# A drain on GpSimd behind every second row gather of a three-layer graph network

## The chip, the core and the metric

The kernel runs on one core of a Trainium2 chip. The metric is the device time of one execution in microseconds (us); lower is better. Engines in the profile: PE is TensorE (PEld its weight loads), DVE is VectorE, ACT is ScalarE, POOL is GpSimd, SP is SyncE. A q behind an engine's name means its sequencer alone.

## The reference

6250 nodes with 256 features each, 100,000 edges sorted by target node, an edge type from 0 to 2, and 32 attributes per edge. Cut to what matters:

```python
ew = edge_attr @ edge_w + edge_b                      # (E, 256)
inv_cnt[i] = 1 / max(segment_sum(edge_type == i, dst), 1)
for l in range(3):
    residual = x
    msg = relu(x[src] * ew)                           # gather one row of x per edge
    out = 0
    for i in range(3):                                # edge types
        h = segment_sum(msg * (edge_type == i), dst) * inv_cnt[i]
        out += h @ weights[l, i]
    x = residual + relu(out + x @ roots[l] + biases[l])
return layernorm(x_input + x)
```

Every layer gathers 100,000 rows of 1 KB from the x that the layer before has written. No layer can start its gathers before the last rows of x are stored.

## The kernel before, in words

The edges are cut into 782 tiles of 128 edges. One tile is one gather: a single indirect DMA, issued by GpSimd, that takes 128 row numbers from `idx` and brings 128 rows of 256 float32 from HBM into one of 12 slots of the tile `xg` in SBUF. Two tiles make a pair, and the pair is the step of the loop: 391 pairs per layer, 1173 in all, 2346 gathers.

For each pair q the engines do this, in this order:

- PE computes the edge factors of both tiles into PSUM (line 781, four matmuls with 128x256 outputs).
- DVE multiplies the gathered rows by them in place (line 1088). It waits first for the two gathers of the pair (one semaphore per slot, `s_g`) and for PE (`s_e`).
- ACT applies relu in place (line 685).
- PE sums the messages per node and type with one-hot selectors `S` (line 800, eight records per pair), and counts the tile as used on the semaphore `s_sc`.
- DVE adds the two results to the running sums `acc` (line 971).

When the sums of a block of 128 nodes are complete (49 blocks per layer), PE multiplies them with the layer's weights (line 849), DVE adds bias, means and residual (lines 988, 995, 1013), and SP stores the new rows (line 541). Layer 0 also transposes the edge attributes and counts edges; layer 2 also does the layernorm.

No scheduler is at work: each engine runs its own hand-written program, and semaphores join them. GpSimd's program is nearly nothing but gathers. The gather n waits until the tile n-12, which had its slot, has been used by line 800; that wait has the same value for both gathers of a pair, so only the first of them can be held by it. Twelve gathers are issued ahead of the branch into the main loop, then come a few memsets (lines 615 to 622), then the others. At the start of layers 1 and 2 GpSimd waits for the stores of x (`s_xo`, line 628).

In the same queue as the gathers there is nothing else. The other transfers (edge attributes, node blocks, weights, stores) are issued by SP.

Of the kernel before, what the change touches and what calls it, by code (L numbers as in the profile page):

```python
# [59 lines left out]
def gnn_program(nc, x_in, src, dst, edge_attr, edge_type, weights, roots, biases, edge_w, edge_b, due, out):  # L60
# [30 lines left out]
    xs = [x_in, x1, x2, out]  # L91

    order, _, _, blocks, starts, first = plan()

    def rows(k):
# [12 lines left out]
    with ctx:  # L108
# [60 lines left out]
        def c3(p):  # L169
            return p.rearrange("q (c p) -> q c p", p=128)  # L170
# [42 lines left out]
        def uses(l, i, depth, per):  # L213

            return len(range(i, l * per, depth))

        def tile(n):

            return 4 * order[n // 4] + n % 4
# [246 lines left out]
        def both(eng, name, fast):  # L466

            eng.wait_ge(s_flag, 4)
            late = eng.value_load(flag[0:1, 0:1], min_val=0, max_val=128 * 128 * CH + 128 * CH)
            with eng.If(late == 0):  # L470
                fast()
            with eng.Else():
                general(eng, name)
# [112 lines left out]
        @block.gpsimd  # L586
        def _(eng):
            eng.memset(c3(p_src)[:, CH - 1, :], 0).then_inc(s_pad, 1)
            eng.memset(c3(p_dst)[:, CH - 1, :], PAD).then_inc(s_pad, 1)
            eng.memset(c3(p_typ)[:, CH - 1, :], 0).then_inc(s_pad, 1)  # L590
            eng.memset(zcol[:, :], 0.0).then_inc(s_zc, 1)
            eng.memset(p_ew, 0.0).then_inc(s_ez, 1)
            eng.memset(ident[:, :], 0.0).then_inc(s_id, 1)
            eng.wait_ge(s_id, 1)
            eng.affine_select(out=ident[:, :], in_=ident[:, :], compare_op=ALU.not_equal, fill=1.0,
                              base=0, pattern=[[-1, 128]], channel_multiplier=1).then_inc(s_id, 1)
            eng.iota(iota[:, :], [[1, 148]], base=-1, channel_multiplier=0,
                     allow_small_or_imprecise_dtypes=True).then_inc(s_cst, 1)
            eng.memset(ones[:, :], 1.0).then_inc(s_cst, 1)
            eng.memset(mask[:, :], HIGH).then_inc(s_cst, 1)  # L600
            eng.memset(eps[:, :], 1e-5).then_inc(s_cst, 1)
            eng.memset(accf[:, Z[0]:Z[1]], 0.0).then_inc(s_z0, 1)

            def gather(l, j):
                n = l * NT + j
                if n >= XR:
                    eng.wait_ge(s_sc, 2 * ((n - XR) // 2 + 1))
                eng.indirect_dma_start(  # L608
                    out=xg[:, n % XR, :], out_offset=None, in_=xs[l],
                    in_offset=bass.IndirectOffsetOnAxis(ap=idx[:, tile(j):tile(j) + 1], axis=0)).then_inc(s_g[n % XR], 16)  # L610

            eng.wait_ge(s_idx, 2)
            for j in range(XR):
                gather(0, j)
            eng.memset(diff[:, :], 0.0).then_inc(s_df, 1)
            for i, (fill, b) in enumerate(((0.5, 0), (-0.5, 1), (0.5, -127))):
                eng.wait_ge(s_df, i + 1)
                eng.affine_select(out=diff[:, :], in_=diff[:, :], compare_op=ALU.not_equal, fill=fill,
                                  base=b, pattern=[[-1, 128]], channel_multiplier=1).then_inc(s_df, 1)
            eng.memset(accf[:, Z[4]:Z[5]], 0.0).then_inc(s_z0, 1)  # L620
            eng.wait_ge(s_pc, 3)
            eng.memset(accf[:, Z[5]:Z[6]], 0.0).then_inc(s_z0, 1)

            def fast():
                for l in range(L):
                    if l:
                        for i in range(TB):
                            eng.wait_ge(s_xo[i], 16 * uses(l, i, TB, NB))
                    for j in range(0 if l else XR, NT):
                        gather(l, j)  # L630

            both(eng, "gpsimd", fast)
# [245 lines left out]
        def _(eng):  # L878
# [191 lines left out]
            def fast():  # L1070
                for l in range(L):
                    todo = {}
                    for q in range(-6, end):
                        Q = l * NP + q
                        if 0 <= q < NP and q % 2 == 0:
                            w, c = min(4, NT - 2 * q), tile(2 * q)
                            row, c = 32 * (c // BR), c % BR
                            _, vals = nc.values_load_multi_w_load_instructions(  # L1078
                                brow[row:row + 1, c:c + w], engines=[DVE], min_val=0, max_val=R * (N - 1),
                                skip_runtime_bounds_check_because="three times a node's number")  # L1080
                            bases.update({2 * q + i: v for i, v in enumerate(vals)})
# [59 lines left out]
```

## Time and profile before

| what | us |
|---|---|
| median of 3 timed runs | 3098.7 |
| lowest and highest of them | 3095.48, 3101.99 |
| profiled execution, first to last instruction (span) | 3632.0 |
| PE busy in the span | 2818.6 |
| POOL busy in the span | 2256.5 |
| DVE busy in the span | 2148.2 |
| ACT busy in the span | 1285.0 |

The span is all that is recorded of the profiled execution's own time; what lies around it isn't given. It is 533 us longer than the median of the timed runs. Every duration of a single instruction comes from that slower execution. Busy time is the sum of an engine's instruction spans; for a gather, POOL's span is the writing of the transfer's descriptors, not the transfer. Waits are listed as idle time before an instruction, with what ended it; "issue" means that nothing which the profile shows was waited for.

### The profile page before, as it was taken

The numbers are of one execution on the slowest core, as the hardware profiler recorded it, in microseconds if no ns is written. First come the engines' busy times: TensorE is split into PE (matmuls) and PEld (weight loads), VectorE is DVE, ScalarE is ACT, GpSimd is POOL, SyncE is SP. The second block draws the span as 40 slices with busy tenths as digits, with TensorE's granted clock in tenths as the row PEclk, the third lists the DMA queues.
The fourth block names the chain that finished last, engine by engine and source line by source line (L and its number), as shares of the span: only waits on it lengthen the run. The fifth ranks groups of instructions, "written<-read, shape, count | busy, mean of one in ns | idle before, by whom it ended". The sixth has DMA issues, their size and how long they took to land.

```text
span 3632.0 us, 59677 instructions
## 1 busy us (share of the span) xinstructions
PE 2818.6 (78%) x18430; PEld 2609.9 (72%) x18430; DVE 2148.2 (59%) x5997; ACT 1285.0 (35%) x2700; POOL 2256.5 (62%) x2368
## 2 busy tenths in 40 slices
PE   6777778888888777778777877777777777787777
PEld 5777777777777677777777777767666777777776
DVE  6666666666666555555555555545555665556566
ACT  6555555555555322222222222222222222222222
POOL 6666666666666466666666666646666666666664
PEclk9999999999999878888898888887888888888888
DMA  4444444444444344444444444434444444444443
GB/s 126 128 129 128 127 132 127 131 127 131 130 128 130 114 125 118 122 119 121 122 124 118 124 122 119 122 106 127 125 126 121 130 123 127 129 124 130 125 128 100
DMA packets 318631, 450.88 MB, mean 124 GB/s; under 512 B 155996, under 2 KB 205802, under 8 KB 318314
## 3 DMA queue, kind: packets, MB, share of 16 engines
q0 software_dynamic: 112608, 307.65, 29.8%
q1 hardware_dynamic: 205706, 139.36, 13.7%
q8 instruction: 156, 2.56, 0.3%
q14 instruction: 161, 1.32, 0.1%
HBM read 401.96 MB, written 44.82 MB: 123 GB/s over the span
## 4 chain that ended last, share of the span: by engine, by line
PE 61%; issue 16%; another core or an unknown queue 9%; DVE 8%; ACT 3%; DVEq 2%; POOL 1%; DMA 0%; POOLq 0%; SPq 0%
PE bank L800 31%; PE bank L781 14%; PE bank L849 13%; DVE acc L971 4%; PE bank L754 2%; DVE t L988 1%; DVE xg L1088 1%; ACT at L656 1%; PE bank L824 1%; ACT oh_a L702 1%; PE bank L795 1%; DVEq L1078 1%; DVEq L971 1%; DVE S L952 0%
## 5 line engine op out<-in xcount | busy, mean ns | idle before, releaser
L608 POOL DMA_INDIRECT xg<-x,idx x1564 | 1490.9, 953 | 897.3 <-issue 361.5
L800 PE MATMUL bank<-S,xg 128*128 128x96 f32 x9384 | 1459.0, 305 | 400.7 <-issue 197.4
L800 PEld LDWEIGHTS bank<-S,xg 128*128 128x128 f32 x9384 | 1324.2, 217 | 461.2 <-issue 441.2
L685 ACT ACTIVATE xg<-xg 128x512 f32<-128x512 f32 x1173 | 739.1, 630 | 2064.0 <-DVE xg L1088 1270.0
L971 DVE TENSOR_TENSOR acc<-acc,bank 128x192 f32 x2346 | 817.1, 348 | 767.0 <-PE bank L800 490.6
L1088 DVE TENSOR_TENSOR xg<-xg,bank 128x512 f32<-128x512 f32 x1173 | 802.0, 684 | 600.2 <-remote 273.5
L781 PE MATMUL bank<-wsb,at 128*128 128x256 f32 x4692 | 990.4, 338 | 213.8 <-issue 128.8
L608 POOL DMA_INDIRECT xg<-in_x_dram,idx x782 | 750.5, 960 | 451.0 <-PE bank L800 212.2
L781 PEld LDWEIGHTS bank<-wsb,at 128*128 128x128 f32 x4692 | 753.8, 214 | 286.7 <-issue 183.5
L849 PE MATMUL bank<-W,acc 128*128 128x256 f32 x1764 | 506.5, 411 | 2.2 <-issue 2.0
L849 PEld LDWEIGHTS bank<-W,acc 128*128 128x128 f32 x1764 | 385.5, 257 | 5.6 <-issue 2.0
L952 DVE TENSOR_TENSOR S<-iota,kr 128x384 f32<-128x384 bf16 x588 | 324.4, 552 | 0.2
L702 ACT ACTIVATE oh_a<-iota,lo 128x128 bf16<-128x128 bf16 x782 | 267.6, 389 | 69.3 <-PE bank L800 62.8
L988 DVE SCALAR_TENSOR_TENSOR t<-bank,inv,t 128x256 f32<-128x256 f32 x441 | 209.8, 476 | 19.2 <-remote 14.7
L849 PE MATMUL bank<-W,xT 128*128 128x256 f32 (+1 forms) x588 | 195.0, 464 | 0.0
L754 PE MATMUL bank<-ident,hs 128*64 128x128 f32 x782 | 126.1, 284 | 45.8 <-issue 40.4
L795 PE MATMUL bank<-oh_b,oh_a 128*128 128x12 bf16 x782 | 80.0, 174 | 101.1 <-issue 98.2
L795 PEld LDWEIGHTS bank<-oh_b,oh_a 128*128 128x128 bf16 x782 | 52.0, 105 | 132.3 <-issue 113.8
L849 PEld LDWEIGHTS bank<-W,xT 128*128 128x128 f32 (+1 forms) x588 | 125.7, 234 | 14.2 <-issue 0.3
L754 PEld LDWEIGHTS bank<-ident,hs 128*64 128x64 f32 x782 | 86.7, 122 | 58.0 <-issue 56.1
L656 ACT ACTIVATE at<-bank 64x512 fp32r<-64x512 f32 x196 | 113.1, 577 | 42.3 <-remote 32.7
L709 ACT ACTIVATE acc<-zcol 128x768 f32<-128x768 f32 (+1 forms) x98 | 81.7, 834 | 37.3 <-remote 21.7
(87 smaller groups left out, 728.2 us busy)
## 6 DMA issues: line engine op xcount, KB each, us to landing
at<-attr_t SPq DMA_DIRECT2D x390, 128.0 KB
xg<-x,idx POOLq DMA_INDIRECT x1564
attr_t<-at SPq DMA_DIRECT2D x195, 128.0 KB
xg<-in_x_dram,idx POOLq DMA_INDIRECT x782
hs<-in_edge_attr_dram SPq DMA_DIRECT2D x195, 64.0 KB
x<-t SPq DMA_DIRECT2D x96, 128.0 KB
xblk<-x SPq DMA_DIRECT2D x96, 128.0 KB
xblk<-in_x_dram SPq DMA_DIRECT2D x48, 128.0 KB
```

The source lines that it names most:

```text
L608: eng.indirect_dma_start(out=xg[:, n % XR, :], out_offset=None, in_=xs[l], in_offset=bass.IndirectOffsetOnAxis(ap=idx[:, tile(j):tile(j) + ...
L685: eng.activation(v, v, ACT.Relu).then_inc(s_r, 1)
L702: eng.activation(oh_a[:, j % AR, :], iota[:, 1:129], ACT.Sign, bias=lo[:, tile(j):tile(j) + 1]).then_inc(s_oh, 1)
L754: last = eng.transpose(pT[0:64, 128 * i:128 * i + 128], hs[:, g % 3, i, :], ident[:, :])
L781: last = eng.matmul(pE[Q % 2][:, 256 * i:256 * i + 256], at[:, sl, c:c + 128], wsb[:, p, :], start=(p == 0), stop=(p == 1))
L795: eng.matmul(pA[V % 2][:, 384:384 + HW], oh_a[:, (2 * V + i) % AR, :], oh_b[:, slot(l, 2 * q + i), :], start=(i == 0), stop=(i == 1))
L800: last = eng.matmul(pA[V % 2][:, 192 * i + 96 * h:192 * i + 96 * h + 96], xg[:, n % XR, 128 * h:128 * h + 128], S[:, slot(l, 2 * q + i), : ...
L849: last = eng.matmul(o, a, W[:, 2 * (r % 4) + h, :], start=(h == 0), stop=(h == 1))
L952: eng.tensor_tensor(S[:, at4:at4 + w, :], iota[:, 1:WK + 1].unsqueeze(1).to_broadcast([128, w, WK]), kr[:, c:c + w].unsqueeze(2).to_broadc ...
L971: eng.tensor_tensor(a, a, pA[V % 2][:, 192 * i:192 * i + 192] .rearrange("p (h w) -> p h w", h=2), ALU.add).then_inc(s_acc, 1)
L988: return eng.scalar_tensor_tensor(tt, products(k, m), inv[0:n, 3 * blocks[k] + r:3 * blocks[k] + r + 1], tt, ALU.mult, ALU.add)
L1088: eng.tensor_tensor(v, v, pE[Q % 2][:, :].rearrange("p (i d) -> p i d", i=2), ALU.mult).then_inc(s_m, 1)
```

## The change

GpSimd's `gather` gets two lines. Behind every gather with an odd running number, thus once per pair, GpSimd executes a drain instruction. It is not tied to any semaphore. Nothing else is altered; no instruction moves on any engine, and the other engines' programs are the same.

```diff
                 eng.indirect_dma_start(
                     out=xg[:, n % XR, :], out_offset=None, in_=xs[l],
                     in_offset=bass.IndirectOffsetOnAxis(ap=idx[:, tile(j):tile(j) + 1], axis=0)).then_inc(s_g[n % XR], 16)
+                if n % 2:
+                    eng.drain()
 
             eng.wait_ge(s_idx, 2)
             for j in range(XR):
```

The line numbers of the profile are those of the kernel before; the added lines stand behind line 610. `gather` is called for the twelve gathers ahead of the main loop too, so there are 1173 drains: six ahead of the memsets of lines 615 to 622, and 1167 behind them.

## Rows read from the trace of the kernel before

**Rows 1.** The page, busy time of each engine in the whole span.
```profile
PE 2818.6 (78%) x18430; PEld 2609.9 (72%) x18430; DVE 2148.2 (59%) x5997; ACT 1285.0 (35%) x2700; POOL 2256.5 (62%) x2368
```

**Rows 2.** POOL's waits: who waited for whom, us in total, times, longest.
```profile
POOL xg L608 <- issue: 537.8, 1749, 0.7
POOL xg L608 <- PE bank L800: 466.7, 409, 2.3
POOL xg L608 <- remote: 295.2, 185, 2.9
POOL xg L608 <- DMA x<-t: 45.0, 2, 23.1
```

**Rows 3.** Timeline of POOL in layer 1: start, duration, instruction, idle before.
```profile
2004.20 0.95 POOL L608 DMA_INDIRECT xg<-x,idx  x1 [0.30 <-issue]
2005.45 0.95 POOL L608 DMA_INDIRECT xg<-x,idx  x1 [0.30 <-issue]
2006.70 0.95 POOL L608 DMA_INDIRECT xg<-x,idx  x1 [0.30 <-issue]
2008.98 0.94 POOL L608 DMA_INDIRECT xg<-x,idx  x1 [1.33 <-PE bank L800]
2010.23 0.95 POOL L608 DMA_INDIRECT xg<-x,idx  x1 [0.30 <-issue]
```

**Rows 4.** Timeline of DVE at the end of layer 2.
```profile
3605.29 0.68 DVE L1088 TENSOR_TENSOR xg<-xg,bank 128x512 f32<-128x512 f32 x1
3607.15 0.69 DVE L1088 TENSOR_TENSOR xg<-xg,bank 128x512 f32<-128x512 f32 x1
3609.20 0.68 DVE L1088 TENSOR_TENSOR xg<-xg,bank 128x512 f32<-128x512 f32 x1
3611.05 0.69 DVE L1088 TENSOR_TENSOR xg<-xg,bank 128x512 f32<-128x512 f32 x1 [0.25 <-issue]
```

**Rows 5.** Timeline of POOL around the first turn of a layer.
```profile
1217.01 0.94 POOL L608 DMA_INDIRECT xg<-in_x_dram,idx  x1 [0.30 <-issue]
1239.81 0.94 POOL L608 DMA_INDIRECT xg<-x,idx  x1 [21.86 <-DMA x<-t]
1241.06 0.95 POOL L608 DMA_INDIRECT xg<-x,idx  x1 [0.30 <-issue]
1242.31 0.95 POOL L608 DMA_INDIRECT xg<-x,idx  x1 [0.30 <-issue]
1243.56 0.95 POOL L608 DMA_INDIRECT xg<-x,idx  x1 [0.30 <-issue]
1244.82 0.95 POOL L608 DMA_INDIRECT xg<-x,idx  x1 [0.30 <-issue]
1246.07 1.04 POOL L608 DMA_INDIRECT xg<-x,idx  x1 [0.30 <-issue]
```

**Rows 6.** Timeline of DVE behind it: the layer's first three multiplies.
```profile
1245.13 0.69 DVE L1088 TENSOR_TENSOR xg<-xg,bank 128x512 f32<-128x512 f32 x1 [10.34 <-DMA xg<-x,idx]
...
1246.40 0.69 DVE L1088 TENSOR_TENSOR xg<-xg,bank 128x512 f32<-128x512 f32 x1
1248.94 0.69 DVE L1088 TENSOR_TENSOR xg<-xg,bank 128x512 f32<-128x512 f32 x1 [1.85 <-DMA xg<-x,idx]
```

**Rows 7.** Instructions of the program's end: count, duration in ns, start.
```profile
L108 POOLq DRAIN  x1: 10670/10670/10670, 3603.9 to 3603.9; - x1
L108 PEldq DRAIN  x1: 68/68/68, 3620.4 to 3620.4; - x1
L108 ACTq DRAIN  x1: 164/164/164, 3624.2 to 3624.2; - x1
```

**Rows 8.** Timeline of POOL at the program's end.
```profile
3605.18 0.94 POOL L608 DMA_INDIRECT xg<-x,idx  x1 [0.30 <-issue]
```

**Rows 9.** Instructions of the program's first line: count, duration in ns, start.
```profile
L1128 POOLq DRAIN  x1: 187/187/187, 0.4 to 0.4; - x1
```

**Rows 10.** Timeline of POOL before and behind the memsets.
```profile
12.32 1.22 POOL L608 DMA_INDIRECT xg<-in_x_dram,idx  x1 [3.72 <-DVE idx L903]
...
28.95 0.22 POOL L615 MEMSET diff<- 128x128 f32 x1
...
36.94 0.96 POOL L608 DMA_INDIRECT xg<-in_x_dram,idx  x1 [0.15 <-issue]
```

**Rows 11.** Timeline of PE at the start of layer 1.
```profile
1245.96 1.20 PE L781 MATMUL bank<-wsb,at 128*128 128x256 f32 x4 [3.58 <-DVE xg L1088]
1246.96 1.85 PE L800 MATMUL bank<-S,xg 128*128 128x96 f32 x8
```

**Rows 12.** The page, costliest groups: count, busy us, mean ns, idle before.
```profile
L849 PE MATMUL bank<-W,acc 128*128 128x256 f32 x1764 | 506.5, 411 | 2.2 <-issue 2.0
...
L849 PE MATMUL bank<-W,xT 128*128 128x256 f32 (+1 forms) x588 | 195.0, 464 | 0.0
L754 PE MATMUL bank<-ident,hs 128*64 128x128 f32 x782 | 126.1, 284 | 45.8 <-issue 40.4
L795 PE MATMUL bank<-oh_b,oh_a 128*128 128x12 bf16 x782 | 80.0, 174 | 101.1 <-issue 98.2
```

## The prediction, made before the changed kernel had run

> **What bounds the kernel now.** I read the page's busy times first [rows 1]. There PE looks like the bound with 78%, and POOL with 62% seems to have room. That view misleads here, because a gather's 0.95 us is not all that it costs POOL. The timeline of POOL shows it [rows 3]: gathers that wait for nothing start 1.25 us apart, 0.95 us of writing descriptors and 0.30 us of idle time called "issue", so the shortest period of a pair is 2.50 us. The profiled execution takes some 3.0 us per pair, and the waits tell where the rest goes [rows 2]: in 409 + 185 cases POOL waited for PE or for an unnamed releaser, 762 us in all, and 45 us for stores at the two turns of a layer. So in the profile POOL is held by the 12 slots, and the consumers set the pace.
>
> The timed runs are 533 us shorter than the span. I take away what isn't pairs: 12.3 us until the first gather, 8.0 us of memsets (28.95 to 36.94) [rows 10], two turns of 21.9 us [rows 5] and 25.9 us behind the last gather (3632.0 - 3606.1) [rows 8]. That leaves 3098.7 - 90 = 3009 us for 1173 pairs, 2.56 us each. This is 0.06 us over POOL's own 2.50 us. The consumers can be faster than that: at the end of layer 2, where all rows are there, multiplies follow each other in 1.86, 2.05 and 1.85 us [rows 4]. So in the timed runs POOL's queue is nearly saturated, and whatever is put into it counts in full past 0.06 us per pair; in the profiled execution past some 0.5 us.
>
> **The change, and what one drain costs.** It adds 1173 drains and moves nothing. Behind each drain in POOL's queue stands the next pair of gathers, and for them wait DVE's multiply, then ACT, PE and the sums. The question is what the drain waits for. No drain stands behind a gather in a loop in this trace, so I bound it by the three rows that are nearest.
>
> - Lower bound: the drain at the program's start [rows 9] took 187 ns, and all of POOL's work there was memsets of some 0.1 us. A drain that costs the queue only the time of an empty one: 0.05 to 0.19 us.
> - Landing: the drain waits until the rows of both gathers have arrived. How long that is can be read at the start of layer 1, where DVE waits for the rows. The second pair's gather ends at 1243.56 + 0.95 = 1244.51 and its multiply starts at 1246.40, 1.89 us later. The third pair's ends at 1247.11 and its multiply starts at 1248.94, 1.83 us later. The first pair takes 1245.13 - 1242.01 = 3.12 us, with the layer's other loads under way [rows 5, 6]. I take 1.85 us.
> - Upper bound: the closing drain of POOL ran from 3603.9 for 10.67 us, until 3614.5 [rows 7]. The last gather had finished its descriptors at 3606.1 [rows 8], and nothing but drain stood in the queue. So this drain waited 8.4 us behind the last descriptors. The drains of PE and ACT at the same place took 68 and 164 ns [rows 7], so it is not the place that makes it long.
>
> The closing drain is the only one behind gathers, and it excludes that a POOL drain ends with the descriptors: it stayed at least as long as rows need to land. It stayed 6.5 us longer still (8.4 - 1.9), and why I can't read. It came behind 2346 gathers with no drain between, the drains of the change come behind two. I read the excess as settling what had piled up, and expect next to nothing of it behind a single pair. That is the weakest choice here.
>
> The Trainium skill speaks against this. Its page Perfetto Trace Analysis, section DMA Instruction — SWDGE (GPSIMD), lets the GpSimd instruction complete when its cores have written the descriptors, before the data moves; a drain that waits for the engine's instructions alone would by that rule return at once. VectorE: DVE Perf Modes, section The DRAIN you can't avoid, calls the drains around a program boilerplate of about 12 ns on all five engines. By these two the sum would stay at 3098.7 us. The closing drain of 10.67 us does not agree with either.
>
> **The sum.** Period of a pair with a drain: 1.25 us from the first gather's start to the second's, 0.95 us for the second's descriptors, 1.85 us until landing, 0.05 us for the drain to notice, and 0.35 us until the next gather starts (the 0.30 us of issue, and 0.05 us since it can't be prepared during the wait). That is 4.45 us. The slots don't hold POOL then: 12 of them cover 6 pairs, and the consumers need 2 us for what arrives every 4.45. Nothing hides the wait, because the drain stops the very queue that sets the pace.
>
> 1173 x 4.45 = 5220 us. Around it: 12.3 us until the first gather, 8.0 us of memsets. The turns: today 21.86 us between the last descriptors of a layer and the next gather [rows 5]. At the end of layer 2 the last multiply starts 4.9 us behind the last descriptors (3611.05 - 3606.12) [rows 4, 8]; with the drain only 1.9 us, since no backlog is left, so a turn shrinks by 3.0 to 18.8 us, of which 2.25 us are in the pair's period already: 16.6 us, twice 33. The tail: 25.9 - 3.0 - 2.25 = 20.6 us. Sum: 5220 + 12 + 8 + 33 + 21 = 5294, and I say 5290 us. That is 1660 us over the profiled span and 2190 us over the median of the timed runs. I expect span and timed runs to lie close together this time, since what made the profiled execution slow sat with the consumers, and they have room now. The 0.95 and 1.25 us I carry over to the timed runs because their 2.56 us per pair leaves no place for a slower POOL. The landing time might be shorter without the profiler; 0.35 us less would give 4880 us. With 0.5 us more (the first pair's 3.12 us in one case of two) it is 5880 us. The forecast's own range is 4880 to 5880.
>
> **Rivals.**
>
> *The drain ends with the descriptors and hides.* It costs POOL at most the 0.06 us of room per pair, beside waits of 1.33 us for PE as at 2008.98 [rows 3]. Time 3099 us, not slower. The point from which it decides: a drain below 0.06 us. For it speaks the start's drain, most of whose 187 ns lay over the memsets; against it the closing drain. 5%, and 1% for a kernel that even gains since descriptors come in pairs with a rest.
>
> *The drain ends with the descriptors, but breaks the queue.* It costs 0.19 us [rows 9] per pair, 0.13 us past the room: 3098.7 + 1173 x 0.13 = 3250 us. 6%.
>
> *PE falls to its lower clock and becomes the bound.* PE would be busy 2 of 4.45 us and might be granted 1.2 instead of 2.4 GHz. At the start of layer 1, after its 3.58 us of idle time, four matmuls of line 781 took 1.20 us and eight of line 800 took 1.85 us [rows 11]. The blocks' matmuls are (506.5 + 195.0) / 1173 = 0.60 us per pair at the mixed clock [rows 12], up to 1.2 us at the lower: 4.25 us in layers 1 and 2, which just fits. Layer 0 adds (126.1 + 80.0) / 391 = 0.53 us, up to 1.05 us: 5.3 us, 0.85 over POOL's period, times 391 = 332 us. Total 5620 us. [...] 6%.
>
> *Every drain costs what the closing one did.* Period 1.25 + 0.95 + 8.41 + 0.35 = 10.96 us, total 12,930 us. For it speaks the only row of its kind. 4%.
>
> **Chances.** Waiting for the landing 78%, with the low clock on top 6%, 8.4 us each 4%, cheap but visible 6%, hidden 5%, gain 1%. A measurement of this kernel can tell 0.2% (6 us) from no change. So slower 94%, same 5%, faster 1%. The range 4850 to 5950 us holds the first two; I leave out the others.
>
> **What would show it.** In the profile after: 1175 POOL drains (1173 and the program's own two) with a median near 4.2 us, as the sequencer is at the drain before the gathers ahead of it have run (the closing one began at 3603.9, ahead of the gather of 3605.18 [rows 7, 8]); gathers in twos, 1.25 us apart, then 3.2 us to the next start; POOL's waits for PE gone; DVE's multiply waiting for the gather's DMA in nearly every pair, where it now does so at the layers' starts; a pair's period of 4.45 us in all three layers alike; a closing drain that has shrunk from 10.67 to about 3 us. A period that differs between layer 0 and the others would speak for PE's clock. The prediction is wrong if drains end within 0.2 us of the second gather's descriptors, or if they outlast the landing by far more than 0.1 us.

## The result, and the profile after

The changed kernel takes 6049.4 us (median of 4 runs, 6046.9 to 6051.3), the kernel before 3100.3 us in the same runs. The ratio is 1.954, 95% interval 1.951 to 1.957. Forecast were 5290 us with a range of 4850 to 5950 us: the direction and the mechanism held, the size did not.

The one profiled execution of the kernel before was itself slower than its timed runs (3632 against 3100 us), while every other kernel's profile here, of the changed one too (6049.1 us), agrees with its timed runs within 0.1%.

The page of the changed kernel: its span, the busy time of each engine and the granted clock in 40 equal slices, in tenths of full speed. They answer to [rows 1].

```profile
span 6049.1 us, 60850 instructions
PE 4052.7 (67%) x18430; PEld 3424.2 (57%) x18430; DVE 2146.5 (35%) x5997; ACT 1268.8 (21%) x2700; POOL 2234.4 (37%) x2368
...
PEclk7676766777777666666666666666566666666666
```

The clock row of the kernel before:

```profile
PEclk9999999999999878888898888887888888888888
```

POOL's, DVE's and ACT's busy times have not changed by more than 2%. POOL does the same work and stands still in between. PE's matmuls became longer, 4053 us in place of 2819 us, at a lower granted clock: 0.66 of full speed on average, where the profile of the kernel before had 0.895. Both are mixtures of the two levels, 1.2 and 2.4 GHz.

The drains of the loop: count, then shortest, median and longest duration in ns, then the first and the last start in us.

```profile
L612 POOLq DRAIN  x1173: 3421/3899/8920, 12.1 to 6023.2; - x196
```

The waits of the changed kernel: who waited for whom, us in total, times, longest. They answer to [rows 2].

```profile
ACT xg L687 <- DVE xg L1090: 4743.5, 1170, 22.6
POOL xg L608 <- issue: 3376.7, 2208, 5.5
DVE xg L1090 <- issue: 1868.3, 601, 5.4
DVE xg L1090 <- DMA xg<-x,idx: 1472.0, 409, 11.1
...
DVE xg L1090 <- DMA xg<-in_x_dram,idx: 496.6, 157, 4.1
...
POOL xg L608 <- PE bank L802: 367.3, 135, 3.6
```

DVE's multiply (now line 1090) waits 3837 us in all, in 1167 of 1173 cases, and it starts 0.08 us behind the landing of its rows in nearly all of them, also where the profile says "issue". In kernel 1 below, whose profile shows what the timed runs of the kernel before do, it waited 859 us for them, of which the largest part is this:

```profile
DVE xg L1091 <- DMA xg<-x,idx: 404.6, 370, 11.1
```

POOL's idle time ahead of gathers is put down to "issue", since a drain has no semaphore by which the profile could name it. The "PE bank L802" among POOL's waits is a trap: the sums that the gather waits for have ended at least 6.2 us before it starts (22 us in the median), and only the same semaphore happened to be updated by a later pair near the end of the drain.

One pair of the changed kernel, timeline of POOL, and of DVE behind it: start, duration, idle before. They answer to [rows 3] and [rows 6].

```profile
2810.86 0.94 POOL L608 DMA_INDIRECT xg<-x,idx  x1 [3.62 <-issue]
2812.11 0.94 POOL L608 DMA_INDIRECT xg<-x,idx  x1 [0.30 <-issue]
2815.65 0.94 POOL L608 DMA_INDIRECT xg<-x,idx  x1 [2.60 <-issue]
```

```profile
2814.89 0.69 DVE L1090 TENSOR_TENSOR xg<-xg,bank 128x512 f32<-128x512 f32 x1 [3.11 <-issue]
```

The second gather has its descriptors written at 2813.05. At 2814.89, 1.84 us later, its rows are there and DVE starts. At 2815.65, 0.76 us behind that, POOL writes again. Over all pairs the trace's records of the semaphores give the terms, as means: landing 2.05 us behind the descriptors (median 1.85, one in ten over 2.70), drain's end 0.115 us behind the landing, next gather 0.76 us behind the drain's end (median 0.73; the mean holds the two waits at the turns of a layer). The middle term is the finding: while the landing varies from 1.71 to 4.65 us, the drain's end stays 0.114 to 0.116 us behind it in nearly all pairs and 0.125 us at the most.

The program's closing drain, answering to [rows 7]:

```profile
L108 POOLq DRAIN  x1: 55/55/55, 6027.7 to 6027.7; - x1
```

It took 10.67 us before and 55 ns now, with the last pair already drained.

### The profile page after: what moved, and what is told of

Same layout as the page of the kernel before. It is cut to its first block, busy times and chain, and to the rows that moved or that the text cites. A ratio compares the mean times of both kernels' runs of the same rounds, so it can differ in the third digit from the quotient of the medians.

```text
span 6049.1 us, 60850 instructions
## 1 busy us (share of the span) xinstructions
PE 4052.7 (67%) x18430; PEld 3424.2 (57%) x18430; DVE 2146.5 (35%) x5997; ACT 1268.8 (21%) x2700; POOL 2234.4 (37%) x2368
## 3 DMA queue, kind: packets, MB, share of 16 engines
q8 instruction: 156, 2.56, 0.2%
## 4 chain that ended last, share of the span: by engine, by line
PE 29%; issue 29%; DMA 24%; POOL 7%; DVE 6%; POOLq 3%; ACT 2%; DVEq 0%
PE bank L802 17%; DMA xg<-x,idx 15%; PE bank L783 9%; DMA xg<-in_x_dram,idx 8%; POOL xg L608 7%; DVE xg L1090 5%; POOLq L612 3%; PE bank L851 2%; ACT at L658 1%; PE bank L756 1%; DVE acc L973 0%; PE bank L797 0%; PE bank L826 0%; DVEq L1088 0%; ACT xT L695 0%
## 5 line engine op out<-in xcount | busy, mean ns | idle before, releaser
L783 PE MATMUL bank<-wsb,at 128*128 128x256 f32 x4692 | 1210.3, 399 | 1562.8 <-DVE xg L1090 1338.0
L802 PE MATMUL bank<-S,xg 128*128 128x96 f32 x9384 | 1965.2, 378 | 121.8 <-DVE acc L973 75.7
L783 PEld LDWEIGHTS bank<-wsb,at 128*128 128x128 f32 x4692 | 923.2, 273 | 1936.3 <-issue 850.6
L802 PEld LDWEIGHTS bank<-S,xg 128*128 128x128 f32 x9384 | 1770.9, 282 | 216.7 <-ACT xg L687 144.6
L851 PE MATMUL bank<-W,acc 128*128 128x256 f32 x1764 | 664.8, 516 | 2.5 <-DVE t L990 2.5
L851 PEld LDWEIGHTS bank<-W,acc 128*128 128x128 f32 x1764 | 458.7, 293 | 43.7 <-DVE t L990 2.8
L851 PE MATMUL bank<-W,xT 128*128 128x256 f32 (+1 forms) x588 | 252.3, 575 | 0.0
L756 PE MATMUL bank<-ident,hs 128*64 128x128 f32 x782 | 172.6, 364 | 89.6 <-ACT xT L695 89.6
L826 PE MATMUL bank<-ident,xblk 128*128 128x128 f32 (+1 forms) x294 | 83.7, 382 | 116.7 <-ACT at L658 116.7
L826 PEld LDWEIGHTS bank<-ident,xblk 128*128 128x128 f32 (+1 forms) x294 | 53.3, 211 | 142.5 <-issue 138.5
```

The lines of the kernel that those rows point to most:

```text
L756: last = eng.transpose(pT[0:64, 128 * i:128 * i + 128], hs[:, g % 3, i, :], ident[:, :])
L783: last = eng.matmul(pE[Q % 2][:, 256 * i:256 * i + 256], at[:, sl, c:c + 128], wsb[:, p, :], start=(p == 0), stop=(p == 1))
L802: last = eng.matmul(pA[V % 2][:, 192 * i + 96 * h:192 * i + 96 * h + 96], xg[:, n % XR, 128 * h:128 * h + 128], S[:, slot(l, 2 * q + i), : ...
L851: last = eng.matmul(o, a, W[:, 2 * (r % 4) + h, :], start=(h == 0), stop=(h == 1))
```

## The experiments

Their terms are read in the same way, from the traces' semaphore records. "L" is the theory that a drain waits for the landing of the gathers ahead of it.

**Is it the landing?** First, a wait for the same landing in place of the drain.

```diff
                 if n % 2:
-                    eng.drain()
+                    eng.wait_ge(s_g[n % XR], 16 * (n // XR + 1))
```

> In place of each drain GpSimd waits on the semaphore that tells of the second gather's landing; no drain in the loop. Theory L (a drain holds the queue until the rows of the gathers before it have landed, 2.05 us behind the descriptors on average in the changed kernel, then ends 0.12 us later, and the empty queue needs 0.76 us to the next gather): the landing stays, and only the restart can be cheaper, since the next gather is prepared while it waits. Period 1.25 + 0.95 + 2.05 + 0.3 to 0.5 us = 4.55 to 4.75 us, total 5400 to 5650 us. Rival F (a drain has a fixed price of some 2.9 us of its own, which has nothing to do with the landing): the wait costs the landing all the same, so this run alone does not tell L and F apart; it is the base for the next one.

5512.6 us; ratio to before 1.787 (1.784 to 1.790). Timeline of POOL:

```profile
2803.43 0.94 POOL L608 DMA_INDIRECT xg<-x,idx  x1 [0.30 <-issue]
2807.46 0.94 POOL L608 DMA_INDIRECT xg<-x,idx  x1 [3.09 <-DMA xg<-x,idx]
```

This lies inside the expected 5400 to 5650 us. Now the profile can name the releaser. The landing took 2.17 us on average, and the next gather started 0.26 us behind it (median), where with a drain it starts 0.84 us behind it (0.115 + 0.73). Less the 0.12 us that the landing took longer, 0.46 us per pair are left, or 540 us. That is what was measured: of the changed kernel's loss of 2949 us, 2430 us are the wait for the landing alone, and 537 us come with the drain as an instruction (the two series' own runs of the kernel before differ by 18 us). Next, the wait and then the drain.

```diff
                 if n % 2:
+                    eng.wait_ge(s_g[n % XR], 16 * (n // XR + 1))
                     eng.drain()
```

> GpSimd first waits for the landing of the second gather, and then executes the drain, when nothing is in flight on its queue. L: the drain finds nothing to wait for and ends in some 0.1 us; total within 2% of the changed kernel, 6000 to 6150 us. F: 2.9 us on top of the landing, period 7.2 to 7.5 us, total 8500 to 8900 us.

6210.2 us, ratio 2.014 (2.010 to 2.018), 1% above the range of L and far from F's.

```profile
L613 POOLq DRAIN  x1173: 198/198/225, 17.4 to 6184.4; - x196
```

With nothing of its own queue in flight each drain takes 0.198 us, 225 ns at the most. The fixed price F has fallen. At the start of 217 of these drains one of SP's loads or stores was on its way, and 109 times it was still on its way when the drain ended; each of these drains took 0.198 us. So a GpSimd drain waits for GpSimd's transfers and not for all.

**How does it grow with the number of gathers?** Only the condition was changed.

```diff
-                if n % 2:
+                if n % 4 == 3:        # n % 16 == 15, n % 64 == 63, n % 256 == 255; in one kernel no condition
                     eng.drain()
```

> Drain behind every fourth gather. L: four gathers take 3 x 1.25 + 0.95 + 2.05 + 0.12 + 0.76 = 7.63 us, times 586.5 = 4475 us, with about 75 us around it 4550 us. Rival P (a drain's price grows with the number of gathers since the last one, 1.3 to 1.45 us each): the total stays near 6000 us.

> Drain behind every gather. L: 0.95 + 2.05 + 0.12 + 0.76 = 3.88 us per gather, times 2346 = 9100 us, with what is around it 9170 us. P: near 6000 us, since the price per gather is the same.

> Drain behind every 16th gather. L without backlog (the drain costs the same 0.12 to 0.2 us behind the landing, however many gathers came before): 16 gathers take 15 x 1.25 + 0.95 + 1.95 + 0.2 + 0.77 = 22.6 us where they take 20.5 us in before's timed runs, so 146.6 drains add at most 2.1 us each: 3400 us at most, and less where the slots' backlog hides part. Rival B (a drain settles each gather since the last drain, some 0.04 us each by what every second, every fourth and a drain behind a wait show): its end lies 0.7 us behind the landing.

> Drain behind every 64th gather, 36 of them. L without backlog: end 0.12 to 0.2 us behind the landing. B: 0.04 x 64 = 2.8 us behind it. Time 3100 to 3250 us.

> Drain behind every 256th gather, 9 of them. B without a limit: 11 us behind the landing. B with a limit (entries are settled at other times too): about the 5.9 us that the closing drain of before ended behind the last landing. L without backlog: 0.2 us. Time 3090 to 3150 us in each case.

| drain behind every | time us | ratio (95%) | drains | rise per drain, timed, us | POOL's idle behind it, less 0.30 us | end behind the landing, us |
|---|---|---|---|---|---|---|
| gather | 8554.1 | 2.774 (2.769 to 2.780) | 2346 | 2.33 | 2.39 | 0.07 |
| 2nd (the change) | 6049.4 | 1.954 (1.951 to 1.957) | 1173 | 2.51 | 2.63 | 0.115 |
| 4th | 4513.9 | 1.464 (1.461 to 1.467) | 586 | 2.44 | 2.60 | 0.20 |
| 16th | 3550.9 | 1.150 (1.148 to 1.153) | 146 | 3.17 | 3.19 | 0.69 |
| 64th | 3292.4 | 1.067 (1.065 to 1.069) | 36 | 5.66 | 5.74 | 3.26 (2.7 to 3.6) |
| 256th | 3131.9 | 1.015 (1.013 to 1.017) | 9 | 4.81 | 4.79 | 2.37 (2.2 to 2.6) |

The fifth column is (time minus the kernel before in the same call) / drains, the sixth the mean idle time between the descriptors of the gather ahead of the drain and the start of the next, less the 0.30 us that stand there anyway. They agree within 0.2 us in every row: what a drain costs POOL is what it costs the kernel. Theory P (a price per gather) has fallen with the first three rows, where time goes with the number of drains. L gave 4550 us for every fourth (4514 measured) and 9170 us for every gather (8554 measured). Behind every 16th and every 64th gather the drains cost more than I had expected: 3551 us against at most 3400 by L without a pile, and 3292 us against 3100 to 3250. The second is 7% too high, as the landing of a single gather was shorter (1.88 us against 2.05) and the terms behind it smaller by 0.07 us.

The last column bears on what I had left to judgement. The drain's end moves with what has piled up since the last one, by 0.041 to 0.043 us for each gather: 0.07, 0.115, 0.20 and 0.69 us for 1, 2, 4 and 16. The closing drains of the same runs fit too: 1.76 us behind the last landing where 42 gathers had come since the last drain. At 64 the steps would give 2.7 to 2.8 us, measured were 2.7 to 3.6 us; at 256 they stop growing (2.4 us), against my 11 us without a limit and 5.9 us with one. The closing drain of the kernel before, behind all 2346, ended 5.6 us behind the last landing, and those of the four other kernels here without a drain in the loop 6.1, 6.2, 7.2 and 8.6 us, with the same number of gathers. So in these the number of gathers does not set the time. What limits the pile, why 256 gave less than 64, and what the closing drains of these five do, is open.

Timeline of POOL with a drain behind every 64th gather: it stands between the two rows, and POOL idles 6.00 us. The releaser named is the trap from above.

```profile
2946.07 0.95 POOL L608 DMA_INDIRECT xg<-x,idx  x1 [0.30 <-issue]
2953.02 0.94 POOL L608 DMA_INDIRECT xg<-x,idx  x1 [6.00 <-PE bank L802]
```

**What are the 0.73 us (0.76 us in the mean) behind a drain?** A small memset was put behind each drain. The diff is cut: the memset's tile and its semaphore are left out, and the wait is told in a comment.

```diff
                 if n % 2:
                     eng.drain()
+                    eng.memset(spare[:, n // 2 % 8:n // 2 % 8 + 1], 0.0).then_inc(s_sp, 1)   # and a wait that has long ended
```

> The changed kernel, and behind each drain one memset of a column of a spare tile. It splits the 0.76 us from a drain's end to the next gather's start. Q (the sequencer restarts an empty queue, a price of any instruction): the memset starts 0.4 us or more behind the drain and the gather soon after it. G (it is what the gather itself needs until its record starts): the memset starts 0.1 to 0.2 us behind the drain, the gather at about 0.76 us as before. Time 6050 to 6100 us.

6087.7 us, ratio 1.966 (1.962 to 1.970). Timeline of POOL:

```profile
2800.38 0.95 POOL L610 DMA_INDIRECT xg<-x,idx  x1 [0.30 <-issue]
2803.43 0.10 POOL L617 MEMSET spare<- 128x1 f32 x1 [2.10 <-issue]
2804.12 0.94 POOL L610 DMA_INDIRECT xg<-x,idx  x1 [0.59 <-issue]
```

The memset started 0.07 us behind the drain's end in the median, the gather at 0.76 us where it was 0.73 us without the memset; these 0.03 us are the 38 us that the kernel became slower. So it is G: the drain lets go at once, and a gather that is issued into an empty queue needs 0.7 us before its record starts. Behind another gather only 0.30 us show, and behind the semaphore wait of the first experiment 0.26 us. I read this so: the gather is prepared while its forerunner runs or while it waits for a semaphore, and a drain forbids that. No row shows the preparation itself.

**Is POOL the bound of the kernel before?** In three other kernels something else stands in the drain's place. The diff is cut in the same way; kernels 2 and 3 have a small spare tile more.

```diff
                 if n % 2:
-                    eng.drain()
+                    eng.sem_inc(s_sp, 1)                              # kernel 1
+                    eng.memset(spare[:, ...], 0.0)...                 # kernel 2: one column, a ring of 8 (cut)
+                    for i in range(4):                                # kernel 3: each waits for the one before
+                        eng.memset(spare[:, :], 0.0).then_inc(s_sp, 1)
+                        eng.wait_ge(s_sp, 4 * (n // 2) + i + 1)
```

> In place of each drain the sequencer increments an unused semaphore, an instruction that never reaches the GpSimd cores. It tests whether any instruction between the pairs breaks the queue. I expect that it runs beside the gathers, as the sequencer is ahead of them: within 10 us of before. If it broke the queue as the rival with 0.13 us per pair had it: 150 us more.

> In place of each drain GpSimd executes a memset of one column of a spare tile (128x1, 0.09 us in the trace of before); no drain. It tests the claim that POOL's queue has only some 0.06 us of room per pair in the timed runs. Saturated: the memset adds 0.1 to 0.4 us to a period of 2.56 us, of which all but 0.06 counts: 3130 to 3500 us, and then the rise in the profile's period is smaller than in the timed runs. Not saturated (the consumers set the pace in the timed runs too): within 10 us of before.

> In place of each drain four memsets of one column, each waiting for the one before, and the next gather behind them; no drain. One memset fitted into the 0.30 us between two gathers and cost nothing. If POOL's queue sets the pace of the kernel before, a stay of about 0.8 us per pair must count with what exceeds the gap, some 0.4 to 0.8 us: 3550 to 4050 us. If the consumers set it: within 1% of before, about 3100 us.

Kernel 1: 3096.6 us, ratio 0.9996 (0.9984 to 1.0009). An instruction that only the sequencer executes costs nothing here. Its profile spans 3096.8 us, so it shows what the timed runs of the kernel before do. POOL's waits there:

```profile
POOL xg L609 <- issue: 516.8, 1697, 0.3
POOL xg L609 <- PE bank L803: 196.8, 646, 0.3
POOL xg L609 <- DMA x<-t: 37.5, 2, 19.3
```

Behind the first gather no wait but the turns is longer than 0.3 us, the gap between any two gathers. The queue is saturated, with 2.56 to 2.60 us per pair. What this is over 2.50 us is no idle time: the descriptors of a gather take 0.98 us on average here, and 0.95 us in the changed kernel. Kernel 2: 3088.4 us, ratio 0.9998 (0.9985 to 1.0012), against my "3130 to 3500 us if saturated". The timeline shows the memset inside the gap, and the gathers still 1.25 us apart:

```profile
1999.13 0.95 POOL L610 DMA_INDIRECT xg<-x,idx  x1 [0.30 <-issue]
2000.08 0.11 POOL L616 MEMSET spare<- 128x1 f32 x1
2000.38 0.95 POOL L610 DMA_INDIRECT xg<-x,idx  x1 [0.19 <-issue]
```

So this run did not tell the two apart as I had meant it to: small work hides in the gap of 0.30 us. Kernel 3 does tell: 4117.2 us, ratio 1.326 (1.324 to 1.328), above my 3550 to 4050 us.

```profile
2002.56 0.95 POOL L610 DMA_INDIRECT xg<-x,idx  x1 [0.30 <-issue]
2003.51 0.58 POOL L615 MEMSET spare<- 128x1 f32 x4
2004.72 0.95 POOL L610 DMA_INDIRECT xg<-x,idx  x1 [0.62 <-POOL spare L615]
```

The gathers stand 2.16 us apart instead of 1.25 us; 0.91 x 1173 = 1067 us, and the kernel lost 1014 us. If the consumers had set the pace, it would have stayed near 3100 us. A kernel with twelve memsets in this place has no time, since its spare tile did not fit into SBUF.

**Why does the landing take 2.05 us and not 1.85?** In layers 1 and 2 the attribute reload was cut to 16 x 16 numbers; this kernel leaves out the attributes of these layers, so it no longer computes the reference.

```diff
-                w = 128 * tiles_of(g)
-                eng.dma_start(at[0:64, G % TR, 0:w].bitcast(F32), attr_t[g, :, 0:w]).then_inc(s_at[G % TR], 16)
+                eng.dma_start(at[0:16, G % TR, 0:16].bitcast(F32), attr_t[g, 0:16, 0:16]).then_inc(s_at[G % TR], 16)
```

> The changed kernel with its drains, but in layers 1 and 2 the reload of the edge attributes brings 16 x 16 numbers instead of 64 x 512 (the attributes of these layers are left out), so SP's transfers there shrink. Theory S (the landing takes 2.05 us on average instead of the 1.85 us forecast because other transfers are in its way): mean landing in layers 1 and 2 falls from 2.06 us to 1.85 to 1.95 us, 782 x 0.1 to 0.2 us = 80 to 160 us less than the changed kernel, 5890 to 5970 us. Rival: the longer landings belong to the gathers themselves (random rows, 16 queues): no change, 6030 to 6060 us.

5954.5 us, 95 us less than the changed kernel (ratios to before 1.923 and 1.954). The mean landing fell from 2.06 to 1.94 us in layers 1 and 2, and stayed at 2.03 us in layer 0, where nothing was changed. 782 x 0.12 = 94 us. More than half of the excess over 1.85 us in these layers is that one stream of transfers; the rest, among it node blocks and stores, was not taken apart.

## Why the prediction was right or wrong

- *POOL's queue is saturated in the timed runs.* Right, and it rested on a subtraction; kernel 1's profile and kernel 3 show it. There is not even the 0.06 us of room per pair that I had allowed. It explains why each drain counts in full.
- *The drain waits for the landing.* Right: 0.115 us behind it in pair after pair, and 0.198 us where the landing had been waited for.
- *The closing drain's excess is a pile that is settled, next to nothing behind one pair.* Right for what this kernel needed: 0.04 us per gather, 0.115 us behind a pair. That this is also the 5.6 us of the closing drain is not shown, since five closing drains behind 2346 gathers differ by 3 us.
- *The sum.* The step that failed is the period of a pair, 4.45 us forecast and 5.09 us measured; the mechanism was right, and the terms behind the descriptors were too small. Its terms:

| term | forecast | measured | times 1173 |
|---|---|---|---|
| first gather's start to the second's | 1.25 | 1.25 | 0 |
| second gather's descriptors | 0.95 | 0.95 | 0 |
| landing | 1.85 | 2.05 | +235 us |
| end of the drain behind it | 0.05 | 0.115 | +76 us |
| until the next gather starts | 0.35 | 0.73 (without the turns) | +446 us |

Together 757 us; the forecast missed by 759. The largest error is the last term. I took the 0.30 us between gathers in a row for all that a gather needs, and added 0.05 us. But a memset starts 0.07 us behind a drain and a gather 0.73 us, so 0.30 us is only the part that shows while the queue is never empty, and a drain is just what empties it. The landing was taken from two quiet moments; the mean has a tail, partly SP's attribute loads. The range had room for one such error (0.5 us) but put it on the landing alone. Its upper bound was also worked out too low: 3.12 us in one case of two is 0.64 us over 1.85 us and not 0.5 us, which would have given 6040 us. Even this would have been nearly right for a wrong reason, since the mean landing is 2.05 us and not 2.49 us.
- *What lies around the pairs: 74 us.* Right: 6049.4 - 1173 x 5.09 = 79 us.
- *Span and timed runs close together.* Right, 6049.1 and 6049.4 us. The reason that I gave can't be claimed, since kernels 1 and 2, with the consumers as busy as before, agreed with their timed runs too.
- *PE's lower clock becomes the bound.* It did not, though the granted clock fell to 0.66 on average. Eight matmuls of line 802 take 1.9 to 2.0 us at many places, and DVE still waits for rows in all layers; the periods are 5.06, 5.10 and 5.11 us, the shortest in layer 0, where PE has the most to do and where this rival asked for 5.3 us.
- *The drain ends with the descriptors.* Fallen in both forms, and with it, for GpSimd, the boilerplate of about 12 ns in VectorE: DVE Perf Modes of the Trainium skill, section The DRAIN you can't avoid. In the kernels of this case GpSimd's closing drain took 49 ns to 18.0 us. That of kernel 1 began far ahead of the gathers that it waited for:

```profile
L108 POOLq DRAIN  x1: 17822/17822/17822, 3064.9 to 3064.9; - x1
```

- *4.2 us as the drains' median.* Roughly: 3.9 us, with 4.10 us as the mean. There are 1175 drains, as forecast.
- *A closing drain of about 3 us.* Wrong: it took 55 ns. The loop's last drain stands behind the last pair and had already waited for it.
- *3.2 us from the second gather's start to the next one.* Wrong with the sum: 3.9 us on average (0.95 + 2.93).

No version here beats the kernel before. It stands at the pace of its gathers, and nothing that was tried makes a gather cheaper.

## What to carry to other kernels

In these kernels a drain on GpSimd is a wait for every gather that it has issued, not a cheap marker: behind transfers in a loop it makes their latency part of the loop, 2.6 us each time here. If an order has to be kept, wait on the transfer's semaphore instead: directly behind the gather it cost 0.5 us less per pair. A later wait should cost less still, but none was measured. And price a stall of a queue by what an instruction needs when nothing runs beside it, not by the gap between two in a row.

## What the runs showed of the hardware that I had not expected

- A gather of 128 rows of 1 KB needs 0.73 us from an ended drain to the start of its record on an otherwise empty GpSimd, where a memset needs 0.07 us.
- In the 0.30 us between two gathers a memset of one column runs for nothing (3088.4 against 3088.6 us).
- A drain ends the later behind the landing, the more gathers came since the last one: by 0.041 to 0.043 us each, up to 42; at 64 and 256 it is no longer in proportion (3.3 and 2.4 us in all).
